# Cross attention: another order of the rows that pass through DRAM, and a later rounding of the context rows

## The reference

```python
q = (text_hidden @ Wq).reshape(B, T_text, N_HEADS, HEAD_DIM).transpose(0, 2, 1, 3)   # 16 heads of 128
k = (vision_tokens @ Wk).reshape(B, T_vis, N_KV_HEADS, HEAD_DIM).transpose(0, 2, 1, 3)
v = (vision_tokens @ Wv).reshape(B, T_vis, N_KV_HEADS, HEAD_DIM).transpose(0, 2, 1, 3)
scores = jnp.einsum('bhtd,bhsd->bhts', q, k) / scale
attn = jax.nn.softmax(jnp.where(mask, scores, -jnp.inf), axis=-1)
out = jnp.einsum('bhts,bhsd->bhtd', attn, v)
x = _layernorm(x + out.transpose(0, 2, 1, 3).reshape(B, T_text, N_HEADS * HEAD_DIM) @ Wo)
```

## Time and profile before

| | |
|---|---|
| median of the runs | 2041.88 us |
| the profiled execution | 2043.21 us |
| its span, first to last instruction | 2041.4 us |
| mean granted clock of TensorE | 0.93 |
| busy share of PE, DVE, ACT, POOL | 81%, 65%, 50%, 51% |
| moved by DMA | 341.48 MB |
| stores of a unit, fetches of a unit | 128 and 128, 768 KB each |

### The profile page before, as it was taken

How to read it: one execution, slowest core, us unless ns; L and a number is a source line. 1 busy time by engine, 2 the same in 40 slices (tenths; PEclk the granted TensorE clock), 3 DMA queues, 4 the chain that set the end, 5 groups by cost and what they waited for, 6 DMA issues and landing times.

```text
span 2041.4 us, 25874 instructions
## 1 busy us (share of the span) xinstructions
PE 1651.4 (81%) x8498; PEld 1409.2 (69%) x8498; DVE 1332.2 (65%) x3134; ACT 1020.0 (50%) x1780; POOL 1038.6 (51%) x726
## 2 busy tenths in 40 slices
PE   8999678787878787878787878787878787859897
PEld 7898567666766676767666767666666676648896
DVE  6456766766676766666666666666666667637447
ACT  5443455555454555455555555545555555434452
POOL 1110455655555555555655565555555555343635
PEclk9999889899988899989998999998989999979899
DMA  4346577777786877777777777777777775743333
GB/s 167 107 142 210 189 192 175 197 178 189 169 189 168 188 176 182 174 182 176 183 172 184 176 185 181 176 174 182 181 176 180 177 180 149 156 143 96 93 97 101
DMA packets 188865, 341.48 MB, mean 167 GB/s; under 512 B 41118, under 2 KB 151360, under 8 KB 188608
## 3 DMA queue, kind: packets, MB, share of 16 engines
q1 hardware_dynamic: 146800, 316.81, 60.9%
q10 hardware_dynamic: 38912, 14.80, 3.6%
q0 software_dynamic: 3024, 8.26, 1.5%
HBM read 214.28 MB, written 125.55 MB: 166 GB/s over the span
## 4 chain that ended last, share of the span: by engine, by line
PE 28%; DMA 26%; DVE 15%; issue 7%; ACT 6%; SPq 4%; POOL 3%; DVEq 0%; ACTq 0%; POOLq 0%
DMA b_c_raw<-in_ctx 18%; DVE b_by_block L1085 6%; DMA p_store<-b_by_block 6%; PE b_out L911 4%; ACT b_p L970 3%; PE b_out L912 3%; PE b_out L913 3%; SPq L801 3%; PE b_score L863 3%; PE b_score L865 3%; PE b_score L864 3%; DVE b_p L1066 3%; PE b_out L922 2%; POOL b_keyed_over L1237 2%; PE b_turn L877 2%
## 5 line engine op out<-in xcount | busy, mean ns | idle before, releaser
L1237 POOL TENSOR_TENSOR b_keyed_over<-b_keyed,b_pT_hi 125x512 fp32r<-125x512 f32 x372 | 467.0, 1289 | 309.7 <-ACT b_pT_hi L963 309.7
L1066 DVE CUSTOM_DVE_ANT_0 b_p<-b_score,b_mask_add 128x500 f32<-128x500 f32 x672 | 445.6, 670 | 254.6 <-PE b_score L865 249.2
L970 ACT ACTIVATE b_p<-b_p,b_shift 128x1500 f32<-128x1500 f32 x224 | 347.4, 1551 | 94.9 <-DVE b_top_min L1075 94.9
L895 PE MATMUL b_out<-b_pT_hi,b_c_hi 125*128 125x384 f32 x384 | 173.4, 452 | 265.1 <-DVE b_pT_lo L1090 263.6
L1085 DVE STREAM_TRANSPOSE b_by_block<-b_p 128x1536 f32<-128x1536 f32 x128 | 372.9, 2913 | 9.6 <-DMA p_store<-b_by_block 9.6
L1090 DVE TENSOR_TENSOR b_pT_lo<-b_turn,b_pT_hi 125x384 fp32r<-125x384 f32 x384 | 210.3, 555 | 257.8 <-ACT b_pT_hi L956 251.4
L956 ACT CAST b_pT_hi<-b_turn 125x384 fp32r<-125x384 f32 x384 | 179.7, 477 | 251.2 <-PE b_turn L877 246.1
L863 PE MATMUL b_score<-b_cT_hi,b_q_hi 128*128 128x500 f32 x672 | 276.9, 412 | 17.3 <-DVE b_top L1066 9.5
L895 PEld LDWEIGHTS b_out<-b_pT_hi,b_c_hi 125*128 125x128 f32 x384 | 78.6, 205 | 288.3 <-DVE b_pT_lo L1090 284.9
L963 ACT CAST b_pT_hi<-b_keyed 125x512 fp32r<-125x512 f32 x384 | 221.9, 614 | 97.5 <-PE b_out L913 86.4
L864 PE MATMUL b_score<-b_cT_lo,b_q_hi 128*128 128x500 f32 x672 | 269.7, 401 | 0.0
(11 more groups left out here) (261 smaller groups left out, 3378.1 us busy)
## 6 DMA issues: line engine op xcount, KB each, us to landing
p_store<-b_by_block SPq DMA_DIRECT2D x128, 768.0 KB, 10.7
b_keyed<-p_store SPq DMA_DIRECT2D x128, 768.0 KB
cT_in<-in_ctxT SPq DMA_DIRECT2D x32, 750.0 KB, 6.0
b_c_raw<-in_ctx SPq DMA_DIRECT2D x32, 750.0 KB
q_store<-a_fold_in_or_q_stage SPq DMA_DIRECT2D x16, 896.0 KB, 4.2
q_in<-q_store SPq DMA_DIRECT2D x32, 448.0 KB, 10.2
b_rden_all<-rden_store ACTq DMA_DIRECT2D x32, 256.0 KB, 6.5
b_rden_all<-rden_store ACTq DMA_DIRECT2D x32, 192.0 KB, 10.1
```

The lines of the kernel that those rows point to most:

```text
L895: pe.matmul(out, hi, pT_hi[:, c % 3, 0:w], start=(c == 0), stop=False)
L970: act.activation(own, own, ACT.Exp, bias=shift[:, par, k:k + 1], scale=float(X_SCALE), accum_out=den[:, par, k:k + 1]).then_inc(exp_done, 1)
L1066: dve.tensor_tensor_reduce(out=row(m, u)[:, keys], in0=score_bank[j][:, 0:FW], in1=mask_add[:, b, keys], scale=1.0, scalar=-3.0e38, op0=AL ...
L1237: pool.tensor_tensor(keyed_chunk(keyed_lo, c), keyed_chunk(keyed, c), by_blocks(pT_hi[:, c % 3, :]).bitcast(F32), ALU.subtract).then_inc(k ...
```

## The change

- turn_blocks reads runs of 32 neighbouring keys, where it read steps of 4. So group r of a chunk is now the keys 32r to 32r + 31.
- store_p issues four DMAs for a unit, one for each row group a: 32 partitions, for each of them four pieces of 1.5 KB, which go to where DRAM holds, for key (r, i), all rows of the unit side by side. The semaphore counts 64 for a unit (STORES), where it counted 16.
- load_keyed fetches 128 partitions of one piece of 6 KB each.
- SP's list in a batch: the four load_keyed come first, then load_c, then store_p of unit 0.
- ACT rounds the context rows at step 15, where it was step 8 (C_HI_AT).
- POOL takes the low half of the context rows in three pieces of 512 columns (C_PARTS), behind the keyed chunks 2, 5 and 8 of the same batch; in batch 0 the three follow each other. PE waits for the three.

```diff
-        CT_HI_AT, C_HI_AT = 1, 8
+        CT_HI_AT, C_HI_AT = 1, 15
+        C_PARTS = 3
...
-                sp.dma_start(D["p"][m % 2, u].rearrange("q a n -> q (a n)"),
-                             by_block[:, u % 2].rearrange("q r b j -> q (r b j)")).then_inc(p_stored[u % 2], 16)
+                k = (EVEN * m + u) % 2
+                for a in range(QUADS):
+                    sp.dma_start(D["p"][m % 2, u, :, :, a].rearrange("r i n -> i r n"),
+                                 by_block[32 * a:32 * (a + 1), k].rearrange("q r b j -> q r (b j)")).then_inc(
+                                     p_stored[k], 16)
...
-                sp.wait_ge(p_stored[u % 2], 16 * (EVEN // 2 * m + u // 2 + 1))
+                sp.wait_ge(p_stored[n % 2], STORES * (n // 2 + 1))
                 sp.dma_start(keyed[:, QUADS * u:QUADS * (u + 1), :],
-                             D["p"][m % 2, u].rearrange("(a i) r n -> (i r) a n", a=QUADS)).then_inc(keyed_loaded, 16)
+                             D["p"][m % 2, u].rearrange("r i a n -> (r i) a n")).then_inc(keyed_loaded, 16)
...
             for m in range(B):
+                if m:
+                    for u in range(EVEN):
+                        load_keyed(m - 1, u)
                 if m >= 2:
                     load_c(m)
                 if m:
                     store_p(m, 0)
-                    for u in range(EVEN):
-                        load_keyed(m - 1, u)
...
-                dve.wait_ge(p_stored[u % 2], 16 * (EVEN // 2 * m + u // 2))
+                n = EVEN * m + u
+                if n >= 2:
+                    dve.wait_ge(p_stored[n % 2], STORES * (n // 2))
                 own = row(m, u)
-                keys = bass.AP(own.tensor, own.offset, [own.ap[0], [1, QUADS], [CK, CH], [QUADS, 32]])
-                dve.transpose(by_block[:, u % 2], keys).then_inc(blocks_turned, 1)
+                keys = bass.AP(own.tensor, own.offset, [own.ap[0], [32, QUADS], [CK, CH], [1, 32]])
+                dve.transpose(by_block[:, n % 2], keys).then_inc(blocks_turned, 1)
...
-            def c_rest(m):
-                b = m % 2
-                pool.wait_ge(c_hi_done, m + 1)
-                pool.tensor_tensor(c_lo[b][:], c_raw[b][:], c_hi[b][:].bitcast(F32), ALU.subtract).then_inc(c_lo_done, 1)
+            def c_rest(m, part):
+                b, cols = m % 2, slice(part * CH * CD // C_PARTS, (part + 1) * CH * CD // C_PARTS)
+                if part == 0:
+                    pool.wait_ge(c_hi_done, m + 1)
+                pool.tensor_tensor(c_lo[b][:, cols], c_raw[b][:, cols], c_hi[b][:, cols].bitcast(F32), ALU.subtract).then_inc(
+                    c_lo_done, 1)
```

More of the change, by code:

```diff
@@ L713, in phase_b @@
         BLOCKS_AT = (5, 8, 12, 15)
+        STORES = 16 * QUADS
         RDEN_AT, STORE_AT, LOAD_AT = (15, STEPS + 1), (16, STEPS + 2), (STEPS + 16, STEPS + 8)
@@ L891, in weigh_odd @@
                         pe.wait_ge(oT_done, OT_OPS * (2 * m - 1))
-                    pe.wait_ge(c_lo_done, m + 1)
+                    pe.wait_ge(c_lo_done, C_PARTS * (m + 1))
                 pe.wait_ge(lo_done, CH * m + c + 1)
@@ L1249, in gpsimd @@
                     mask_bias(m + 1)
-                c_rest(m)
-                if m:
+                if m == 0:
+                    for part in range(C_PARTS):
+                        c_rest(0, part)
+                else:
                     for c in range(CH):
@@ L1255, in gpsimd @@
                             rstd((m - 3) // 2)
+                        if c % 3 == 2 and c // 3 < C_PARTS:
+                            c_rest(m, c // 3)
             return lambda b: oT_rest(LAST - 1 + b), lambda: rstd(END)
@@ L1261, in phase_b @@
             fill_done=(fill_done, PFILLS * B), fill_taken=(fill_taken, PFILLS * B),
-            p_stored=[(stored, 16 * EVEN // 2 * B) for stored in p_stored], rden_stored=(rden_stored, 32 * B),
+            p_stored=[(p_stored[k], STORES * (EVEN * B // 2)) for k in range(2)], rden_stored=(rden_stored, 32 * B),
             first_batch_weighed=(pv_done, whole(LAST - 1)), weighed=(pv_done, whole(LAST)),
@@ L2278 @@
     D["rden"] = nc.dram_tensor("rden_store", (B, 2, 128 * EVEN), F32, kind="Internal").ap()
-    D["p"] = nc.dram_tensor("p_store", (2, EVEN, 128, QUADS, ACROSS), F32, kind="Internal").ap()
+    D["p"] = nc.dram_tensor("p_store", (2, EVEN, QUADS, 32, QUADS, ACROSS), F32, kind="Internal").ap()
     D["y2"] = nc.dram_tensor("y2_store", (B * S, F), F32, kind="Internal").ap()
```

## The result

The kernel after takes 2078.33 us (2076.31 and 2080.35) against 2041.88: a ratio of 1.018, interval 1.0125 to 1.0232. On another chip it was 1.030 (1.028 to 1.032, run after_again). The range held the time; the forecast side, faster, was wrong. Ratios are of fast runs; one of the four executions of before_csplit_rden took 3880.93 us and was slow, and is not in its ratio.

A forecast was written before the change was run, and what follows sets the result against it. Bound: ACT's wait for the context load, held by the trickle. L 24 plus tail 24 gives 48 to 48.2 us a batch against 50.5, -2.4 over 29 batches, -70 us: 1973 us (1972 on the median's footing), range 1880 to 2090.

The forecast's parts named there:

- The trickle: Start of a batch: the store of 4-byte reciprocals blocks transfers behind it until about t0 + 7; the change doesn't touch it.
- the load on five engines: Context load uses 5 of 16 DMA engines; 5.4 to 6 us behind the fetches, landing at t0 + 20.
- The wait changes its place: ACT's 11.3 us wait at step 8 goes; DVE waits about 9 us at step 12, the third transpose.
- t0: Issue of a batch's context load, let go when the product of the batch before last has read its last chunk.
- L: Landing of the first unit's store, which the third transpose awaits: t0 + 24, from t0 + 17 to t0 + 28.
- The tail: Steps from L to the next t0: 24.4 us before, sum 23.7, taken as 24, ends 21 and 27.
- The shorter transposes: DVE's transposes: 1.65 us each instead of 2913 ns; two of four lie behind L, so -2.5 us a batch.
- The thirds: POOL's low half of c in three pieces of 1.2 us: +1.3 us a batch, ends 0 and +3.6.
- The granted clock: PE's clock: a 9 us stall brings the half clock, +2.5 us in the steps behind L.
- B: Rival, wait for a wait: fetches contend or stores land late, L t0 + 26.5, then 24; 2041 us, chance 0.24.
- A: Rival, nearly no stall: trickle doesn't hold fetches on all 16 engines, L t0 + 17; 1869 us, chance 0.20.
- C: Rival, slower: narrow stores at half rate become the bound, 53 us a batch; 2115 us, chance 0.21.

The follow-up runs named there:

- before_csplit_rden: Kernel before with the context load split into 112 and 13 partitions and the reciprocals stored in 128-byte pieces; ratio 0.918.
- after_old_layout: Kernel after with the old layout: transposes in steps of 4, one store of 6 KB pieces, fetches of 1.5 KB pieces; ratio 1.070.
- layout_thirds: Kernel before with the new layout and the low half of the context rows in three pieces between keyed chunks; ratio 1.048.
- thirds_norm_late: layout_thirds with DVE's instruction for the second half of the result's norm at step 23, where it was step 19; ratio 1.023.

## Why the prediction was wrong

*What bounds the kernel:* right. The trickle behind the store of reciprocals and the load on five engines are shown by taking them away.

*The wait changes its place:* right in mechanism. The context wait at step 8 is gone and DVE waits at the third transpose, 11.0 us where 9 were forecast. Of the context wait 3.4 us are left at step 15, where under 2 was the sign given: c_hi starts at t0 + 25.4 in the mean, where the sum had the rows landed at t0 + 21.

*L, the landing of the first unit's store:* this is the step that failed, and by its size. Forecast t0 + 24, measured 27.4 in the mean (25.9 on the other chip), and the forecast gain of 2.4 us a batch was smaller than this error of 3.4. In the batch of 1050.65, where the third transpose starts at t0 + 28.3, its parts were:

- The trickle lasted to t0 + 9.4, where the sum had 7. The row it was read from (1036) is already t0 + 7.6, and I had read its end from five engines and one store. About 0.7 us of fetches slipped through, where I had let 1 us pass.
- The fetches then ran to t0 + 17.5, some 8 us, where the sum had them end at t0 + 14.
- The context rows landed at t0 + 26 (c_hi starts at 26.3, straight behind its wait): 8.5 us, where the sum had 6 at most. Until 1074 the DMA share was still 0.9 to 1.1, so the stores and the queries issued behind the load ran beside it; the rate in the sum was that of the load alone.
- The first unit's store and its landing took some 2 us, where the sum had 3.7.

The mean stays within the bound given, t0 + 28. The 400 GB/s of the fetches came out right for a wrong reason: the sum gave it to the pieces of 6 KB, but pieces of 1.5 KB reach it too (396 and 409 GB/s in after_old_layout, with the third transpose at 27.3). What went with the 269 GB/s of before was the load beside them.

*The tail:* 24.4 against 24, within 0.5 us, but two of its terms were off in opposite directions. The shorter transposes gave 2.1 us (26.5 in after_old_layout against 24.4), where the sum had 2.5: they take 1.77 us, not 1.65, and the sum's own rule gives 1.7. The thirds cost 2.2 us in even batches where the tail can be compared (22.8 to 25.0), against 1.3 forecast, and 8.0 in odd ones, by a wait for POOL that was in no part of the sum; the kernel after escapes most of it. The granted clock was at its lower level behind the stall, as forecast (0.50 at 1076 to 1078 and at 1083); what it cost, and what ACT and POOL gained during the stall, no run tells apart.

*The sum:* 27.4 + 24.4 = 51.8 against 50.4 before: +1.4 x 29 = 41 us on 2041.9 is 2083, measured 2078.

*The rivals:* B, a wait for a wait, came nearest: its L of t0 + 26.5 and tail of 24 are the measured ones within 1 us, and its "stores land late" is the half of its condition that held. But it forecast no change. The time is 36 us over before, within the 2% that could not be told from it, yet clear of it by the interval, and 3.0% over on the other chip. A is excluded: wide fetches are held as well (15 GB/s at 1058 to 1060). C's premise has support, since a window with the narrow stores alone moves 249 GB/s at a share of 0.98, where wide ones had 414. The pieces of 1.5 KB are not what makes them slow, since fetches in such pieces had 396 and 409; that it is the 32 partitions is argued, not shown, as no run has stores of this piece size over 128 partitions. But stores did not become the bound, and the layout, narrow stores included, gains 3%.
C drew on the Trainium skill ("SBUF — State Buffer", Door 1: The DMA port swizzle), by which 32 partitions reach half the ports; 249 against 414 GB/s agrees with it roughly. The rule on cachelines of the same page agrees too: 1766 against 2913 ns.

*The choice among the cases:* I set two cases for faster against one of each other sign, with a likeliest value that needed L right within 2.4 us, while its bounds were 11 us apart. A margin smaller than the error of the term it hangs on is no forecast of a sign.

## What to carry to other kernels

When a transfer is late, look first at what is in flight beside it: here stores of 1.5 and 2 KB in 4-byte pieces, on a queue with 3.6% of the engines' time, kept nearly everything else from the 16 engines until 7.6 to 9.4 us into the batch, and cost 8% of the launch. To reorder the transfers behind such a block mostly chooses which engine waits. And before POOL is given more work in an unbroken row, look for instructions of DVE that wait for it: a stretched instruction in the timeline is the sign, and the table of waits doesn't show it.

## What was not expected of the hardware

- A DVE tensor_scalar of 112 x 256 fp32 from SBUF to SBUF lasted 9.96 us beside nine POOL tensor_tensor in a row, and 0.41 us where POOL had a gap. The Trainium skill ("SBUF — State Buffer", SBUF: two separate sides) tells of a port pair that DVE and GpSimd lock for a whole instruction. The traces agree, as each wait ends 0.15 us behind the end of a POOL instruction. Which one it is, they leave open: in layout_thirds and thirds_norm_late DVE was passed over at every boundary of the row (with one exception in nine cases), in the kernel after it got in at the next. DVE's other kinds of instruction ran on beside POOL at their usual length (the transpose 1.77 us with and without POOL).
- A store of 384 pieces of 4 bytes, on a queue that has 3.6% of the 16 engines' time with all else that is on it, kept the other queue's transfers at 0 to 49 GB/s until 7 to 9.4 us after t0. Pieces of 12 bytes, a third as many, did so until 2 to 3 us after it.
- Four DMAs of 32 partitions each, SBUF to DRAM in pieces of 1.5 KB, moved 249 GB/s at a share of 0.98; fetches over 128 partitions in pieces of the same size moved 396 to 409.
- The kernel before varied by 3% over five occasions (1977 to 2042 us), and only by 0.1% on the chip that had it twice (1981 and 1983). The transfer leg of the kernel after varied by 1.5 us a batch between two chips, with the tail the same to 0.1 us.
